# Spreading the max pass of attention more evenly over the key loop, and moving the last layernorm's apply steps of the first token half into the second half's matmul loop

## The reference, cut to what matters

```python
# layer 0: x is (4, 4096, 4096); attention works on it seen with 8 heads of 64
q, k, v = projections of x to 8 heads * 64          # D = 4096 -> 512 each
scores  = einsum('bhqd,bhkd->bhqk', q, k)
attn    = softmax(scores, axis=-1) / sqrt(512)
y       = einsum('bhsl,bhlv->bhsv', attn, v) @ Wo_w.T + Wo_b
x       = layernorm(x + y)
# feed-forward: dense 4096 x 4096 plus top-2 of 8 rank-16 experts
combine = renormalised top-2 of softmax(x @ W_router.T)
lora    = einsum('ner,eor->no', einsum('nd,erd->ner', x, A) * combine, B) * 2
x       = layernorm(x + x @ W_base.T + b_base + lora)
```

## Time and profile before

| | us |
|---|---|
| median of 2 runs (lowest, highest) | 4600.17 (4590.43, 4609.9) |
| the profiled execution, its time | 4633.46 |
| its span on the slowest core (core 3) | 4631.9 |
| spans of the 8 cores | 4508.6 to 4631.9 |

### The profile page before, as it was taken

The page is one execution under the profiler, slowest core; times in us unless marked ns, Lnnn a source line. Parts: engine busy times, 40 slices in busy tenths (PEclk is TensorE's granted clock), DMA queues, the critical chain, the costliest instruction groups (busy, mean ns, idle before and its releaser), DMA issues.

```text
span 4631.9 us, 46121 instructions; the slowest of 8 cores (4508.6 to 4631.9 us)
## 1 busy us (share of the span) xinstructions
PE 3355.1 (72%) x13476; PEld 1206.6 (26%) x13476; DVE 1390.1 (30%) x1908; ACT 833.0 (18%) x1412; POOL 711.2 (15%) x567
## 2 busy tenths in 40 slices
PE   4775996687787887777778745542899960799970
PEld 3563432211111111111111111110344420344430
DVE  0000000355545455455454325552100023100014
ACT  1221000033323233233232311110000000000000
POOL 2112001000000000000000013334222224222225
PEclk9988998666756566566565677775899975899985
DMA  8997445100000000000000042215444538555437
GB/s 248 284 286 232 137 124 176 42 1 1 1 3 1 1 1 3 1 1 1 3 1 1 1 148 73 73 37 168 136 151 152 157 96 198 160 164 152 151 94 187
DMA packets 450638, 444.75 MB, mean 96 GB/s; under 512 B 21472, under 2 KB 402529, under 8 KB 450402
## 3 DMA queue, kind: packets, MB, share of 16 engines
q1 hardware_dynamic: 347490, 341.12, 25.1%
q10 hardware_dynamic: 102912, 100.68, 7.3%
HBM read 340.01 MB, written 100.66 MB: 95 GB/s over the span
## 4 chain that ended last, share of the span: by engine, by line
PE 56%; DVE 10%; DMA 7%; issue 4%; POOL 4%; ACT 0%; DVEq 0%; SPq 0%; POOLq 0%; ACTq 0%
PE pf L155 21%; PE sS L155 10%; PE rb L155 10%; PE a L155 8%; DMA res2c<-r2scr 4%; DVE racc L556 3%; PE po L155 3%; DVE rrec L730 2%; DVE x2g L939 2%; POOL tmpf L929 2%; POOL tmpo L1383 2%; DMA x2h<-x2scr 1%; PE pstQ L155 1%; PE sS L581 1%; PE pstS L155 1%
## 5 line engine op out<-in xcount | busy, mean ns | idle before, releaser
L556 DVE TENSOR_REDUCE racc<-sS 128x1 f32<-128x512 f32 x1024 | 683.2, 689 | 1481.2 <-PE sS L155 1476.0
L155 PE MATMUL pf<-x2h,wqf 128*128 128x512 bf16 x4096 | 909.0, 380 | 5.9 <-DVE hs L1226 5.9
L704 ACT ACTIVATE probs<-rb 128x512 bf16<-128x512 f32 x1024 | 548.6, 597 | 1176.5 <-PE rb L155 1175.9
L155 PE MATMUL sS<-kT,qT 64*128 64x512 bf16 x1024 | 519.4, 534 | 123.0 <-DVE racc L556 62.1
L155 PEld LDWEIGHTS pf<-x2h,wqf 128*128 128x128 bf16 x4096 | 396.5, 98 | 505.3 <-issue 38.5
L155 PE MATMUL a<-probs,V 128*65 128x512 bf16 x1024 | 413.2, 547 | 0.1
L155 PE MATMUL rb<-qT,kT 64*128 64x512 bf16 x1024 | 403.5, 545 | 0.0
L1248 POOL CAST wqf<-wstgf 128x1024 bf16<-128x1024 f32 x256 | 264.7, 1040 | 772.3 <-DMA wstgf<-wbT 438.9
L155 PE MATMUL pk<-xbf,wk_bf 128*128 128x256 bf16 x2048 | 267.7, 292 | 133.6 <-ACT xbf L333 62.3
L1314 DVE SCALAR_TENSOR_TENSOR res2c<-pf,bB_sb,x2h 128x1024 bf16<-128x1024 f32 x64 | 82.2, 1284 | 900.7 <-PE pss L155 827.3
L818 POOL CAST wo_bf<-wstgo 128x1024 bf16<-128x1024 f32 x16 | 16.6, 1040 | 1973.4 <-DMA wstgo<-woT 1973.4
(11 more groups left out here) (104 smaller groups left out, 1868.0 us busy)
## 6 DMA issues: line engine op xcount, KB each, us to landing
wstgf<-wbT SPq DMA_DIRECT2D x256, 512.0 KB
xstg<-xrot SPq DMA_DIRECT2D x128, 512.0 KB
xscr<-xbf ACTq DMA_DIRECT2D x128, 256.0 KB, 5.4
xvb<-xscr SPq DMA_DIRECT2D x128, 256.0 KB, 2.8
outT<-outst ACTq DMA_DIRECT2D x64, 512.0 KB, 6.6
xqb<-xscr SPq DMA_DIRECT2D x32, 512.0 KB, 3.5
xq<-xscr SPq DMA_DIRECT2D x32, 512.0 KB, 3.4
x2scr<-x2g ACTq DMA_DIRECT2D x32, 512.0 KB, 2.8
```

The lines of the kernel that those rows point to most:

```text
L155: return lambda e: e.matmul(o, l, r, start=st, stop=sp, skip_group_check=True)
L556: e.reduce_max(d, srd, AX.X, negate=True),
L704: e.activation(d, srd, AF.Exp),
```

## The change

Two parts.

*Attention.* `pend` becomes one list for each head. At the end of a round, each head's list is emptied down to one matmul if it holds more than two, and there is a `drain_n(1)` behind each head in place of one behind both. So a round has five `drain_n(1)` calls in place of four, 80 units of the next group are issued within a group and only `mk_tdm` is left to `drain_until`; and of a round's `a` matmuls those of its first chunk are issued in the round itself.

*Feed-forward part.* The four instructions of an apply step become a function `emit_apply`, with buffers `res2d` of their own for the load. At the end of a half its 32 steps are only noted in `apply_pend`. In the next half two of them are issued ahead of the loads and casts of each block `wq`; after the last half all are issued in a row.

```diff
                                 drain_until(hp * 4 + qg)
-                                pend = []
+                                pend = [[], []]
...
-                                            pend.append((hx, kc, te, col))
+                                            pend[hx].append((hx, kc, te, col))
                                         drain_n(1)
                                     drain_n(1)
-                                    while len(pend) > 4:
-                                        emit_av(*pend.pop(0))
-                                    drain_n(1)
-                                for item in pend:
-                                    emit_av(*item)
+                                    for hx in range(2):
+                                        if len(pend[hx]) > 2:
+                                            while len(pend[hx]) > 1:
+                                                emit_av(*pend[hx].pop(0))
+                                        drain_n(1)
+                                for hx in range(2):
+                                    for item in pend[hx]:
+                                        emit_av(*item)
...
+            res2d = [sbP("res2d%d" % i, [128, 1024], BF16) for i in range(2)]
+            res2dR = [Res(), Res()]
...
+                apply_pend = []
+
+                def emit_apply(ath, mc, ta2, tb2c):
+                    ri = mc % 2
+                    trl = s.op("SP", lambda e, mc=mc, ath=ath, ri=ri:
+                               e.dma_start(
+                                   res2d[ri][:],
+                                   r2scr_r[:, mc, ath * 1024: ath * 1024 + 1024]),
+                               waits=res2dR[ri].wr() + r2scrR[ath][mc].rd(),
+                               dma="sc")
...
+                    t1 = s.op("POOL", lambda e, d=tmpo[ri][:], a=res2d[ri][:],
+                              b=a2[:]: e.tensor_tensor(d, a, b, ALU.mult),
+                              waits=[trl, ta2] + tmpoR[ri].wr())
...
+                    t2 = s.op("DVE", lambda e, d=outst[ri][:], a=tmpo[ri][:],
+                              b=b2[:]: e.tensor_tensor(d, a, b, ALU.add),
+                              waits=[t1, tb2c] + outstR[ri].wr())
...
                     for wq in range(16):
                         wb = wq % 2
+                        for _ in range(2):
+                            if apply_pend:
+                                emit_apply(*apply_pend.pop(0))
                         for g4 in range(8):
...
+                    ta2, tb2c = tca, tcb
                     for mc in range(NDC):
-                        ri = mc % 2
-                        trl = s.op("SP", lambda e, mc=mc, th=th, ri=ri:
...
+                        apply_pend.append((th, mc, ta2, tb2c))
+                    if th == 1:
+                        while apply_pend:
+                            emit_apply(*apply_pend.pop(0))
```

More of the change, by code:

```diff
@@ L1047, in build_program @@
                 psqR = Res()
+                apply_pend = []
[7 more added lines that the diff above has]
+                               dma="sc")
+                    res2dR[ri].did_write(trl)
+                    r2scrR[ath][mc].did_read(trl)
+                    t1 = s.op("POOL", lambda e, d=tmpo[ri][:], a=res2d[ri][:],
+                              b=a2[:]: e.tensor_tensor(d, a, b, ALU.mult),
+                              waits=[trl, ta2] + tmpoR[ri].wr())
+                    res2dR[ri].did_read(t1)
+                    a2R.did_read(t1)
+                    tmpoR[ri].did_write(t1)
+                    t2 = s.op("DVE", lambda e, d=outst[ri][:], a=tmpo[ri][:],
+                              b=b2[:]: e.tensor_tensor(d, a, b, ALU.add),
+                              waits=[t1, tb2c] + outstR[ri].wr())
+                    tmpoR[ri].did_read(t2)
+                    b2R.did_read(t2)
+                    outstR[ri].did_write(t2)
+                    two = s.op("ACT", lambda e, mc=mc, ath=ath, ri=ri:
+                               e.dma_start(
+                                   outT.ap()[mc * 128: mc * 128 + 128,
+                                             ath * 1024: ath * 1024 + 1024],
+                                   outst[ri][:]),
+                               waits=[t2], dma="out")
+                    outstR[ri].did_read(two)
                 for th in range(2):
@@ L1371, in build_program @@
                     b2R.did_write(tcb)
+                    ta2, tb2c = tca, tcb
                     for mc in range(NDC):
-                        ri = mc % 2
-                        trl = s.op("SP", lambda e, mc=mc, th=th, ri=ri:
-                                   e.dma_start(
-                                       res2c[ri][:],
-                                       r2scr_r[:, mc, th * 1024: th * 1024 + 1024]),
-                                   waits=res2cR[ri].wr() + r2scrR[th][mc].rd(),
-                                   dma="sc")
-                        res2cR[ri].did_write(trl)
-                        r2scrR[th][mc].did_read(trl)
-                        t1 = s.op("POOL", lambda e, d=tmpo[ri][:], a=res2c[ri][:],
-                                  b=a2[:]: e.tensor_tensor(d, a, b, ALU.mult),
-                                  waits=[trl] + a2R.rd() + tmpoR[ri].wr())
-                        res2cR[ri].did_read(t1)
-                        a2R.did_read(t1)
-                        tmpoR[ri].did_write(t1)
-                        t2 = s.op("DVE", lambda e, d=outst[ri][:], a=tmpo[ri][:],
-                                  b=b2[:]: e.tensor_tensor(d, a, b, ALU.add),
-                                  waits=[t1] + b2R.rd() + outstR[ri].wr())
-                        tmpoR[ri].did_read(t2)
-                        b2R.did_read(t2)
-                        outstR[ri].did_write(t2)
-                        two = s.op("ACT", lambda e, mc=mc, th=th, ri=ri:
-                                   e.dma_start(
-                                       outT.ap()[mc * 128: mc * 128 + 128,
-                                                 th * 1024: th * 1024 + 1024],
-                                       outst[ri][:]),
-                                   waits=[t2], dma="out")
-                        outstR[ri].did_read(two)
+                        apply_pend.append((th, mc, ta2, tb2c))
+                    if th == 1:
+                        while apply_pend:
+                            emit_apply(*apply_pend.pop(0))
         s.finish()
```

## The result

The changed kernel takes 4289.2 us in the median where the kernel before takes 4607.5 beside it on the same chip: a ratio of 0.929, 95% interval 0.927 to 0.932, 318 us faster. The forecast was 242 us and 4357. The profiled execution took 4291.8 us.

The account below looks back on a forecast made before the run. PE, in order, was taken to bound attention (mostly at 1.2 GHz) and the feed-forward blocks, idling at group heads and the seam. 4633.5 - 146 + 3 - 99 = 4391.5 us profiled; against timed runs 4600.2 - 242 = 4358, stated 4357, range 4294 to 4418.

Parts of the forecast that it names:

- Step 1: Seam between the feed-forward halves: `x2h` loads no longer queue behind 32 apply steps, 146 us earlier (142 to 147).
- Step 2: Apply steps inside half 1: casts end about 27.7 us after a block's release, within slack; cost 3 us (0 to 60).
- the two ends that the prediction weighed: Half 1, shared SBUF port: `tmpo` up to 2.96 us beside `outst`, or whole-instruction exclusion, 2.5 us a block; same sum.
- Step 3: Attention, what goes: 12.5 us gap at 15 boundaries, `mrow` wait shorter at twelve, longer at three; 189 us gone.
- Step 4: Attention, what comes: units now in the rounds add 4.0 us a group at 1.2 GHz, about 8 at 2.4; 90 us.
- Step 5: Clock in attention: mean 0.60, 98 rounds at 2.4 GHz; no change taken, +-30 us.
- a mean clock in attention off 0.60 by more than 0.03: Attention: one of the listed signs that would show the forecast wrong.
- attention did not give nothing: Rival: in attention, pairs cost in the rounds what they cost in the gap, only the seam gains; 4466 us, chance 0.10.
- weights did not come late: Rival: weights come late in half 1, each block 4 us longer, 60 us more; 4415 us, chance 0.12.
- the clock did not stay down: Rival: the clock never rises in attention, 225 us lost; 4583 us, no change, chance 0.05.

Follow-up runs that it names:

- e1: Kernel before with only the feed-forward part of the change, attention as before; 4449 and 4480 us, beside 4594 and 4626 for before.
- e7: Kernel after with four apply steps ahead of each of the first eight blocks of half 1, not two ahead of all sixteen; 4460 and 4485 us.
- e2: Kernel before with only the attention part of the change, feed-forward part as before; 4395 and 4408 us.
- e4: Kernel before with the `a` matmuls in the order of after, still four units a round and the gap at group heads; 4564 and 4573 us.
- e3: Kernel before with five units a round and no run of pairs at group heads, order of the `a` as before; 4426 to 4452 us.
- e5: Kernel before with five units a round only until 64 are issued, so the gap at group heads stays; ratio 0.998 (0.994 to 1.003).
- e6: Kernel after with one more unit in rounds 2 to 9, so that the `mrow` copy is issued earlier; 4523 to 4550 us.
- e9: Kernel after with `a` matmuls two per chunk from chunk 2, eight `probs` buffers a head, second transpose two pairs later; 4562 to 4602 us, ratio 0.994.
- e10: e9 with one number changed: a group's first `a` come at chunk 4, eight in a row; 4296 and 4302 us, ratio 0.934.
- e12: e10 with the bunch of `a` moved to chunk 7, fourteen in a row; 4238.6 us, a single time.
- e14: e12 with the transposes of a finished row behind four pairs of the next row instead of two; 4365 to 4400 us, ratio 0.953.
- e15: e12 with evacuation off PE's path (ACT copies, makes reciprocals), both broadcasts ahead of the bunch, transposes behind four pairs; 4237.6 to 4264.4 us, ratio 0.925.
- e11: e10 with one more unit in rounds 2 to 9 and evacuation off PE's path (ACT copies accumulators, makes reciprocals); 4405 to 4440 us.

## Why the prediction was right where it was, and where it failed

*Step 1, the seam: right.* 146 us forecast, 151 measured on the core it was worked out for; 115 to 151 over the cores, as the seam of before was 167 to 203 us long. It was read from the core with the longest seam, so it is the upper end of what the change gives. e1 shows it alone.

*Step 2, the apply steps in half 1: right.* 3 us forecast, none measured; casts end after 28.1 us for 27.7, DMA share 0.61 for 0.66. e7 shows that the chain is real and where its slack ends: two steps a block fit, four do not. On the shared port the trace decides between the two ends that the prediction weighed: the first `tmpo` of a block, which begins while the second `outst` still has 0.93 us to go, takes 2.92 us, and the second, alone, 2.13. In before, a `tmpo` that began first kept its 2.12 to 2.14 us beside an `outst`, and the `outst` took 1.9 to 2.9 in place of 1.2. So the one that begins second loses about the time of the overlap. Here that is 0.8 us a block, well inside the slack.

*Step 3, what goes: right in the gap, half right at `mrow`.* The gap of 12.5 us went at all boundaries. The wait for `mrow` did not shrink: 37.0 us in place of 33.1. The prediction took the 1.21 us of one boundary for all; in the second half of attention the wait had been 2.8 to 3.2 us, and it stayed at 2.7 to 3.1. At the three pair ends it is 3.8 to 4.9 us now. Some 6 us too good.

*Step 4, what comes: right at each clock.* 6.04 us for a round at 1.2 GHz in the mean over all cores (forecast 5.81 + 4.0/15 = 6.08) and 4.11 at 2.4 GHz (forecast 3.58 + 8/15 = 4.1). It took half of the rounds at either clock, where its own step 5 has 98 of 256 at 2.4 GHz; that is worth some 7 us.

*Step 5, the clock: this failed.* "I take no change, and +-30 us for it." The time at 2.4 GHz rose from 420 to 602 us a core. A round takes 6.04 us at one clock and 4.11 at the other, so 182 us of it hold what takes 267 at 1.2 GHz. The 85 us between them are nearly all of the excess of attention, 190 in the median for 99 forecast. With them the kernel came out at 4289 us, below 4294, the best end of the forecast's own range. The prediction had named the sign, a mean clock in attention off 0.60 by more than 0.03: it is 0.67. e2 has the excess of attention and e1 has not. Of its sources, e4 shows the order alone: 40 us of attention with nothing else changed, H 459. More came with the gap gone: e3 has 167 us for the 99 that steps 3 and 4 make up, H 516, while e5, as full but with the gap, has H 458. The gains in H of e3 and e4, 96 and 39, do not make up the 182 of both together, so a part is theirs jointly; why the gap keeps the clock down is not shown. That the prediction took "fuller" to mean "more clock", or nothing, was the wrong variable: e6 has six units in rounds 2 to 9, and H 106. Its reading of the last group was a hint that it did not follow up: PE busy all the time at 0.50.

The Trainium skill's page "TensorE: Matmul & The Clock Gate" (Part 1) has it that activity releases the half clock. The traces agree only if not every matmul counts alike: e9 and e10 do the same matmuls, PE is busy for 1654 of 1890 us in the one and 1351 of 1621 in the other, and the one with the larger share stays at 0.50. Their idle time is much alike, 236 and 270 us, so waits do not tell them apart either.

What stays open: which of the holes without `a` make the clock fall. Holes of 1.8 to 2.4 us stand at 170 of the 223 falls inside groups in e12, e14 and e15, but 701 more of them passed; the same place fell on one core and not on another. In before and after, holes of some 2.6 us passed at 2.4 GHz in all of 652 cases, so the length alone does not decide. And whether it is the height of the `a` contraction or another property of them that counts was not tried.

The rivals: attention did not give nothing (e2), weights did not come late (e7 shows from where they would), the clock did not stay down. That it could rise was in none of them.

## What to carry to other kernels

Where PE is in order and its clock moves between two levels, treat the clock as a term of the sum, with an experiment that only reorders: list what PE did just before each rise and each fall, and see which kind of matmul stands there. The same matmuls in another order were worth 270 us here (e9, e10), more than each part of the change. And when work is spread over a stream to fill its gaps, ask of each new neighbour what it delays behind it: e6, e11 and e14 each removed a wait and came out slower than the run that they were made from. More stood between their `a` then, which is the likely cause, not one that was shown by itself.

## What was not expected of the hardware

- What stood ahead of a rise was a row of `a`: within some 3 us behind six of them the clock was at 2.4 GHz in 106 of 129 cases (after), behind fourteen in 512 of 512 (e12 to e15), behind two in 1 of 3744 (e9).
- It fell while PE was busy with other matmuls, not only where it waited, and two `a` per chunk kept it up for 51 us at a time (e12), though the same two never raised it there (0 of 615).
- PE busy for 45 of 45 us stays at 1.2 GHz (last group of after), and PE busy for 1577 of 1854 us has 0.53 in e6.
- In the feed-forward stage all eight cores have 0.98 while PE is busy 494 of 510 us, and this fell to 0.84 in e7, with waits of up to 11.1 us.
- Of a `tmpo` on POOL and an `outst` on DVE that overlap, the one that begins second is the longer: 2.92 us for 2.13 behind an overlap of 0.93 (after), while the first keeps its time.
